# A fused attention and expert stage on one core: in TensorE's step, the second layer of an expert is put ahead of the third layer of the expert one back

## The reference

```python
h = einsum('ni,hio->hno', x, W)                        # 8 heads of 32
w = exp(leaky_relu(attn_src[:, src] + attn_dst[:, dst]) - max)
out = segment_sum(w / segment_sum(w, dst)[dst] * h[:, src], dst) + x

h = relu(bn(einsum('bfd,edh->bfeh', x, W1) + b1))      # layer 1, expert e of 8
h = relu(bn(einsum('bfeh,ehk->bfek', h, W2) + b2))     # layer 2
y = einsum('bfeh,ehd->bfed', h, Wo) + bo               # layer 3
out = einsum('bfed,fe->bfd', y, softmax(x @ Wr + br))
```

## Time and profile before

| | us |
|---|---|
| median of three executions | 6956.88 (6955.64 to 6963.28) |
| the profiled execution | 6955.62 |
| its span, first to last instruction | 6953.9 |
| casts of `low_h1`, first to last start | 644.9 to 3946.3 |
| last product of layer 3 in the fused stage | 3955 |

### The profile page before, as it was taken

One profiled execution on the slowest core, in us unless ns is written; L12 is line 12 of the kernel. 1 busy time (PEld: TensorE's weight loads), 2 busy tenths in 40 slices (PEclk: granted clock), 3 DMA queues, 4 the chain that ended last, 5 costly groups with the idle time before them and its releaser, 6 DMA issues. The chain is left out here.

```text
span 6953.9 us, 120698 instructions
## 1 busy us (share of the span) xinstructions
PE 5410.4 (78%) x32110; PEld 4819.8 (69%) x32111; DVE 4435.2 (64%) x11425; ACT 1822.9 (26%) x4253; POOL 4050.3 (58%) x4038
## 2 busy tenths in 40 slices
PE   3427999999999999999999666767676676665887
PEld 2326888888888888888888555555555555554887
DVE  4436888788878787877888444444444454444666
ACT  1301333333333333333333300000000000002554
POOL 0147666666666666666666177777777777773111
PEclk9757999999999999999999877777777777777999
DMA  4545555555455555555555144444444444443221
GB/s 122 159 127 145 139 139 134 141 132 140 131 141 135 137 137 138 136 139 138 134 140 139 38 125 128 126 128 126 128 123 123 122 118 116 118 119 108 75 76 46
DMA packets 655172, 863.42 MB, mean 124 GB/s; under 512 B 283845, under 2 KB 463511, under 8 KB 654122
## 3 DMA queue, kind: packets, MB, share of 16 engines
q0 software_dynamic: 183296, 501.40, 26.8%
q1 hardware_dynamic: 402060, 294.79, 15.3%
q10 hardware_dynamic: 69406, 61.97, 2.7%
HBM read 714.85 MB, written 155.09 MB: 125 GB/s over the span
## 5 line engine op out<-in xcount | busy, mean ns | idle before, releaser
L1228 POOL DMA_INDIRECT m_ring<-tab_a,m_src x1764 | 1965.9, 1114 | 1219.6 <-DMA m_dstb<-dst_p 692.8
L1819 POOL DMA_INDIRECT eb_rows<-tab_b,eb_src x1568 | 1491.8, 951 | 483.6 <-issue 475.9
L1990 PE MATMUL eb_acc<-eb_rows,eb_S 128*128 128x257 f32 x3528 | 1314.0, 534 | 492.8 <-DMA eb_rows<-tab_b,eb_src 477.6
L1990 PEld LDWEIGHTS eb_acc<-eb_rows,eb_S 128*128 128x128 f32 x3528 | 935.2, 280 | 727.5 <-issue 545.3
L1508 PE MATMUL m_acc<-m_V,m_S 128*128 128x264 f32 x3528 | 867.9, 392 | 0.0
L1508 PEld LDWEIGHTS m_acc<-m_V,m_S 128*128 128x128 f32 x3528 | 653.3, 193 | 93.9
L1622 ACT ACTIVATE mh_full<-m_ps,bn_b,bn_s 128x256 f32<-128x256 f32 x784 | 400.0, 561 | 1189.5 <-DVE mh_low L509 942.5
L509 DVE TENSOR_TENSOR mh_low<-mh_full,mh_high 128x512 fp32r<-128x512 f32 x784 | 541.2, 690 | 154.1 <-ACT mh_full L1633 140.6
L1633 ACT ACTIVATE mh_high<-m_ps,bn_b,bn_s 128x256 fp32r<-128x256 f32 x784 | 441.3, 563 | 702.5 <-PE m_ps L521 702.5
L1304 DVE TENSOR_TENSOR m_V<-m_ring,m_V 128x1280 f32<-128x1280 f32 (+1 forms) x392 | 532.5, 1359 | 57.9 <-DVE m_V L1301 0.5
L521 PE MATMUL m_psY<-mWo_low,mh_high 128*128 128x256 f32 x1568 | 350.5, 305 | 255.7 <-issue 240.5
(11 more groups left out here) (348 smaller groups left out, 10716.5 us busy)
## 6 DMA issues: line engine op xcount, KB each, us to landing
m_dstb<-dst_p SPq DMA_DIRECT2D x196, 320.0 KB
m_dstb<-dst_p SPq DMA_DIRECT2D x196, 256.0 KB
buf<-fill SPq DMA_DIRECT2D x49, 771.0 KB
m_ring<-tab_a,m_src POOLq DMA_INDIRECT x1764
eb_rows<-tab_b,eb_src POOLq DMA_INDIRECT x1568, 2.8
xw_stage<-in_L_ffn_w_dram ACTq DMA_DIRECT2D x16, 1024.0 KB, 8.6
over<-b_blank SPq DMA_DIRECT2D x9, 1452.0 KB, 15.1
mOV<-over SPq DMA_DIRECT2D x49, 264.0 KB, 4.4
```

The source lines that it names most:

```text
L1228: gp.indirect_dma_start(out=ring[:, j, :], out_offset=None, in_=scratch["tab_a"], in_offset=bass.IndirectOffsetOnAxis(ap=src[:, j:j + 1], ...
L1819: gp.indirect_dma_start(out=rows_[par][:, to, 0:D], out_offset=None, in_=scratch["tab_b"], in_offset=bass.IndirectOffsetOnAxis(ap=index[:, ...
L1990: return nc.tensor.matmul(ps_acc[par][:, 0:NR], S[par][:, j, :], rows_[par][:, j, :], start=start, stop=False)
```

## The change

In step `e` of a group TensorE issues layer 3 of expert `e-1` after layer 2 of expert `e` and ahead of `sum_up`. In step 0 the layer 3 of the last group's expert 7 goes behind the `sum_up` of slot -1. No other engine's list is changed, and no instruction is added or taken away.

```diff
                     hand_out(Slot(q, e + 1))
-                    if e:
-                        layer3(q, e - 1)
-                    elif before:
-                        layer3(q.prev(), NX - 1)
                     if e == 5 and after:
 
                         pe.wait_ge(acc_ok, q.n + 1)
@@
                     if e == 0:
                         sum_up(Slot(q, -1))
+                        if before:
+                            layer3(q.prev(), NX - 1)
                         output_bias(q)
                         layer1(q, 1)
                     layer2(q, e)
                     if e:
+                        layer3(q, e - 1)
                         sum_up(Slot(q, e - 1))
```

## The result

The changed kernel takes 7658.53 us (median of 4, 7646.58 to 7668.52), the kernel before beside it 6956.26 (median of 4). The ratio is 1.101, 95% interval 1.099 to 1.103: 702 us slower. The execution shown here took 7658.5 us, with a span of 7656.8.

What follows compares the result with a forecast made beforehand. Neither TensorE nor VectorE was taken as the bound; they wait for each other in one loop. The profiled run's 6955.6 + 351 (order) + 204 (clock) = 7511 us, 7512 against the median; range 7260 to 7720.

Steps and rivals of the forecast that it cites:

- The loop and its terms: TensorE and VectorE waiting for each other, from step 1 to step 7: 53.8 us, 5.6 more than before.
- Over the group's boundary: From step 7 to step 1 of the next group: 1.5 us more, 0.4 of it from step 0.
- Step 0, at 0.4: Layer 3 of the last expert behind `sum_up`: between nothing and 1.2 us a group reaches layer 2 of expert 0.
- The order: Layer 2 waiting for `low_h1` in the fused stage: 7.1 us a group over 47 groups, 351 us in all.
- The last two groups: Groups without edge work, where `low_h1` stands behind `low_h2` too: 16 x 1.06 = 17 us.
- the clock: TensorE's clock falling oftener behind longer stretches of thin products and idleness: 204 us, bounds 0 and 388.
- 3.4 falls a group: Stretches of TensorE's clock at its lower level: 2.85 a group more than before, 1.52 us each.
- the six: Steps of the eight whose stretch comes to 2.28 us or over, each given a share of 0.57 falls.
- Rival A: The fused stage's loop lengthens and the clock falls no oftener: 7308 us, chance 0.27.
- Rival B: Layer 2 finds `low_h1` ready and TensorE's 237.6 us wait ahead of layer 3 falls away: 6719 us, chance 0.03.
- The covers: `relu2` waiting for layer 3 is covered with 1.0 us to spare, GpSimd's gathers have slack: both cost nothing.

Runs made afterwards that it cites:

- c_filler: The changed kernel with eight extra 256-column products on TensorE ahead of layer 2 in steps 1 to 7: 7435.1 us, 1.069 of the kernel before.
- a4_step0: The kernel before with only the edit of step 0, layer 3 of the last group's expert 7 behind `sum_up`: 1.005 of before, on a slower chip.
- c_h1_first: The changed kernel with VectorE's `low_h1(e)` put ahead of `build(e+2)` in steps 1 to 7: 6871.7 us, 0.988 of the kernel before.

## Why the prediction was right, and where its size was off

**The loop and its terms held.** The steps of the changed kernel that run at the full clock can be set beside the terms: from step 1, 9.35 forecast and 9.33 measured (22 of 47 groups); from 2, 9.08 and 9.23; from 4, 8.04 and 8.08; from 5, 9.35 and 9.34; from 6, 8.19 and 8.33. Step 3, forecast at 9.78, is at the full clock in no group; with the extra products it comes down to 10.0. From step 1 to step 7 that is 54.3 us where 53.8 were forecast and 48.2 were before.

**Over the group's boundary** 1.5 us were forecast, from one group. But here the groups are not alike: in the kernel before, the way from step 7 to step 0 takes 12.6 us behind one group and 15.2 behind the next, in turn, and the group that was read has the longer one behind it. For the shorter kind, the groups in which the clock stays up give 14.81 + 5.64 = 20.45 us from step 7 to step 1 in `c_filler` (8 groups), and 12.63 + 6.10 = 18.73 before (19 groups): 1.7 more. For the longer kind it is 16.59 + 5.64 = 22.23 in `c_filler` (4 groups) and 15.15 + 6.10 = 21.25 before, where nearly all have a low clock: 1.0 more. In the mean that is 1.4, near the forecast. Step 0, at 0.4, was a small miss: 0.7 by `a4_step0`, on a slower chip.

**The order** is then 6.1 + 1.4 = 7.5 us a group for the 7.1 forecast, 352 us over 47 groups and not 334. The last two groups, which carry no edge work, take 26 us longer, where 17 were forecast. So the order has about 378 us and was put at 351.

**The term that was mis-sized is the clock.** The casts of step 0 are 82.7 us apart from group to group, and were 68.3: 14.4 more. Less the order's 7.5, the clock has 6.9, about 324 us in all where 204 were forecast. The two misses, 27 and 120 us, are the 147 us by which the forecast was short. The split is an estimate, since the 1.4 rests on few groups: with 1.0 to 1.7 in its place the clock has 343 to 310 us.

The forecast had 3.4 falls a group at 1.52 us each, a price read off a single one. There are 191 in 47 groups, 4.1 a group. For a single fall the price holds: the way from step 1 to 2 takes 10.83 us with one and 9.34 without, from 4 to 5 it takes 9.57 and 8.08, from 6 to 7 9.81 and 8.35, each time 1.5 us. What had no place in the sum is a fall after which the clock stays low for twice as long. All 27 falls before are equally long; of the 191, 37 are twice that, 36 of them at steps 3 and 4, and there the way from 4 to 5 takes 10.65 us, 2.6 more than without a fall. So the average is 6.9 / (4.1 - 0.57), about 1.9 us a fall. Put together from the steps, 154 x 1.5 + 37 x 2.6 = 327 us, less at most 27 x 1.52 = 41 for the falls before: the 324 lie at the upper end.

The total is consistent with the granted clock: 16.6 us a group at the lower level after, 2.0 before, and 6.9 / 14.6 = 0.47 lost for each us more, where 0.5 would be lost if TensorE had full work in all of it. The guess that each stretch of 2.28 us or more falls with the same chance was wrong in its distribution: behind the holes of steps 1 to 7 the clock is low in 25, 33, 47, 37, 0, 6 and 43 of the 47 groups. That isn't the order of the holes' lengths either (step 3, with 1.91 us, has every group, and step 7, with 2.49, has not); why is left open. Step 6, whose hole the router's products cut to 0.91 us, had been counted among the six.

**Rival A**, the order alone at 7308, is excluded by `c_filler`: extra work can't shorten a loop whose only fault is its order. Its own part is about 6957 + 378 = 7335. **Rival B**, a gain, named the right condition: `low_h1` has to end before TensorE leaves `hand_out`. The change doesn't bring that; one edit of VectorE's order does, and then layer 2 and layer 3 both start without a stop in most steps and the kernel is faster than before.

**The covers held.** The wait of `relu2` for layer 3, 1011 us in the changed kernel, is as long in the fastest one. `c_h1_first`, 700 to 3900 us:

```profile
ACT mh_high L1633 <- PE m_psY L521: 1090.0, 335, 6.5
...
DVE mh_low L509 <- ACT mh_full L1633: 14.6, 50, 1.4
```

The second row is `low_h2`, the one that needs what `relu2` makes: VectorE waits 14.6 us for it in all, 83.9 in the changed kernel and 138.2 before. So the late `relu2` costs next to nothing. The longer wait of the gathers for their indices did not show in TensorE's waits either.

What the Trainium skill, TensorE: Matmul & The Clock Gate, section "A second HAM failure mode: psum-queue depth-cycling", says of short and frequent idleness between groups of matmuls, that it makes TensorE swing between two clocks, holds here: the trace agrees, with holes of 1.5 to 2.5 us (medians of steps 1 to 4 and 7) and a granted clock of 0.90.

## What to carry to other kernels

When two engines hand each other work in a loop, write down for each item which position of the other's list makes it, and change both lists together: a consumer moved forward in one list needs its producer moved forward in the other, or the move uncovers the time between the two producers: 1.06 us here, and the ways from step 1 to 2 and from 4 to 5 grew by 1.05 and 1.07, the others between step 2 and step 7 by 0.45 to 1.75. Here the change alone costs 10%, its counterpart alone 0.3%, and the two together gain 1.2%. Price a hole on TensorE twice, once for its length and once for the work behind it at half clock, and for the second ask also for how long the clock may stay down, since one short fall before the change is no guide to that.

## What the runs showed of the hardware that was not expected

Eight useless products a step made the kernel 227 us faster, by keeping the granted clock at 0.98 where it had been 0.90. And the same kernel before took 6955, 7922 and 8072 us on different chips, where the gathers of one stage moved 126 GB/s on the first and 92 on the last; a gain of 1.2% on the one was nothing on the other.
